# First unit of a two-layer linear-attention kernel: value weight split by ScalarE and GpSimd, film gathered earlier, attention in two column groups

## The reference

```python
xn = _ln(x, ln_w, ln_b)
q = xn @ Wq + bq
k = xn @ Wk + bk + (1.0 - src_mask) * -1000000.0
q = jax.nn.softmax(q.reshape(b, t, h, dh), axis=-1)
k = jax.nn.softmax(k.reshape(b, t, h, dh), axis=1)
v = ((xn @ Wv + bv) * src_mask).reshape(b, t, h, dh)
att = jnp.einsum('bnhd,bnhl->bhdl', k, v)
y = jnp.einsum('bnhd,bhdl->bnhl', q, att).reshape(b, t, d)
emb_out = (jax.nn.silu(emb) @ W_emb + b_emb)[:, None, :]
scale, shift = jnp.split(emb_out, 2, axis=2)
hh = _ln(y, ln2_w, ln2_b) * (1.0 + scale) + shift
hh = jax.nn.silu(hh) @ W_out + b_out
return x + hh
```

## Time and profile before

| what | value |
|---|---|
| median of three runs | 811.47 us (810.06 to 811.48) |
| the profiled execution | 811.12 us |
| its span, first to last instruction | 809.2 us |
| TensorE busy | 766.0 us, 95% |
| VectorE busy | 698.7 us, 86% |
| ScalarE busy | 517.0 us, 64% |
| GpSimd busy | 438.4 us, 54% |
| chain that ended last, by engine | TensorE 80%, VectorE 10%, issue 3%, ScalarE 3%, DMA 2%, GpSimd 1% |
| first unit: start of `attend(0)` | 72.03 us |
| start of `output(0)` | 115.47 us |

### The profile page before, as it was taken

One profiled execution on the slowest core, in us unless ns is written; L12 is line 12 of the kernel. 1 busy time (PEld: TensorE's weight loads), 2 busy tenths in 40 slices (PEclk: granted clock), 3 DMA queues, 4 the chain that ended last, 5 costly groups with the idle time before them and its releaser, 6 DMA issues.

```text
span 809.2 us, 16851 instructions
## 1 busy us (share of the span) xinstructions
PE 766.0 (95%) x6359; PEld 371.6 (46%) x6359; DVE 698.7 (86%) x1421; ACT 517.0 (64%) x1011; POOL 438.4 (54%) x432
## 2 busy tenths in 40 slices
PE   4997979999999999998999999999999999999986
PEld 2445434354444445444454544444454544444442
DVE  6898967798998999999988898888888899888985
ACT  4897763856748687686866685565657476560723
POOL 2475573553856658487563755447265535544352
PEclk9997989999999999999999999999999999999999
DMA  9966497664967759596594939588584939485542
GB/s 320 307 130 187 116 257 220 131 147 135 183 171 139 165 153 183 170 180 173 111 187 119 195 106 175 167 153 200 96 192 117 183 119 182 117 150 139 89 120 79
DMA packets 291201, 130.73 MB, mean 162 GB/s; under 512 B 261392, under 2 KB 261776, under 8 KB 291120
## 3 DMA queue, kind: packets, MB, share of 16 engines
q1 hardware_dynamic: 288384, 125.27, 68.7%
q10 hardware_dynamic: 2736, 4.39, 1.6%
HBM read 47.74 MB, written 16.88 MB: 80 GB/s over the span
## 4 chain that ended last, share of the span: by engine, by line
PE 80%; DVE 10%; issue 3%; ACT 3%; DMA 2%; POOL 1%; SPq 0%; DVEq 0%; ACTq 0%; POOLq 0%
PE ring L529 72%; PE ring L699 3%; PE att_ps L648 2%; DMA sb_ht_parts<-sb_htok 2%; DVE sb_k_or_qt L1021 1%; ACT sb_k_or_qt L1410 1%; DVE sb_q_sum L1080 1%; DVE sb_row_peak L868 1%; DMA sb_x<-in_x 1%; DVE sb_ht_parts L1134 1%; PE att_ps L590 0%; PE film_ps L590 0%; DVE sb_q_max L1054 0%; DVE ring L1051 0%; PE film_ps L599 0%
## 5 line engine op out<-in xcount | busy, mean ns | idle before, releaser
L529 PE MATMUL ring<-sb_w_hi,sb_xt_parts 128*128 128x512 f16 x1024 | 309.0, 379 | 0.0
L529 PE MATMUL ring<-sb_w_lo,sb_xt_parts 128*128 128x512 f16 x512 | 194.0, 379 | 0.0
L529 PE MATMUL ring<-sb_w_hi,sb_ht_parts 128*128 128x512 f16 x512 | 158.3, 384 | 10.0 <-DMA sb_ht_parts<-sb_htok 5.8
L529 PEld LDWEIGHTS ring<-sb_w_hi,sb_xt_parts 128*128 128x128 f16 x1024 | 100.3, 98 | 126.1 <-issue 6.6
L529 PE MATMUL ring<-sb_xt_parts,sb_w_hi 128*128 128x512 f16 x496 | 149.9, 384 | 8.6 <-issue 8.1
L1662 POOL TENSOR_TENSOR sb_htok<-sb_ht_parts,sb_htok 128x512 f16<-128x512 f32 x60 | 75.2, 1275 | 137.7 <-ACT sb_htok L1443 137.7
L1678 POOL TENSOR_TENSOR sb_tanh<-sb_v_or_q,sb_kq_hi 128x512 f16<-128x512 f32 x64 | 74.0, 1157 | 88.2 <-ACT sb_kq_hi L1474 87.6
L529 PE MATMUL ring<-sb_w_lo,sb_ht_parts 128*128 128x512 f16 x256 | 98.3, 384 | 0.0
L529 PE MATMUL ring<-sb_xt_parts,sb_w_lo 128*128 128x512 f16 x248 | 95.2, 384 | 0.0
L529 PEld LDWEIGHTS ring<-sb_w_hi,sb_ht_parts 128*128 128x128 f16 x512 | 50.7, 99 | 71.6 <-issue 9.7
L1467 ACT ACTIVATE sb_v_or_q<-ring,sb_ln_one 128x512 f32<-128x512 f32 x64 | 43.9, 686 | 61.6 <-DVE ring L1056 60.7
(11 more groups left out here) (230 smaller groups left out, 1403.1 us busy)
## 6 DMA issues: line engine op xcount, KB each, us to landing
out<-sb_x SPq DMA_DIRECT2D x14, 1024.0 KB, 4.8
sb_rows_now<-film_rows SPq DMA_DIRECT2D x16, 512.0 KB, 4.4
sb_x<-out SPq DMA_DIRECT2D x8, 1024.0 KB, 5.2
...
```

What stands on the lines that cost most here:

```text
L529: last = nc.tensor.matmul(out, lhs, rhs, start=(n == 0), stop=(n == len(pairs) - 1))
```

## The change

Only the first unit's lists change. V's weight is split as Q's is: ScalarE scales and casts chunks 0 and 1 ahead of the keys' exponents and 2 and 3 behind them, GpSimd makes the low halves, and `split_low(V_)` is gone from VectorE. VectorE folds V's bias and makes `v_scales` ahead of `key_sums`. `turn_film` goes behind value tile 0 and `bound_film` behind value tile 2, with `gather_film` and `film_scales` moved to match; `turn_table` goes ahead of the whole `first_attention`, whose products become two column groups of 64 x 64. `mask_attention` goes ahead of `query_sums`, and `find_scale(0, O_)` and `output_scale(0)` between the two pairs of attended tiles. ScalarE makes query tile 0 whole ahead of `normalise(1)`, which is cut in two; `x_sums(2)` goes behind `copy_table` and `x_squares(2)` behind `high_attention`. GpSimd's `add_bias(0)` goes behind `x_norm(2)`. SP issues the transposes of the queries ahead of those of unit 1's input.

```diff
@@ -332,7 +332,7 @@
...
         w_ready = [sem(f"w_ready{i}") for i in range(LAYERS)]
-        q0_ready, o0_ready = sem("q0_ready"), sem("o0_ready")
+        q0_ready, v0_ready, o0_ready = sem("q0_ready"), sem("v0_ready"), sem("o0_ready")
         consts_ready, emb_tanh_ready, emb_ready, pick_ready = sem("consts_ready"), sem("emb_tanh_ready"), sem("emb_ready"), sem("pick_ready")
@@ -438,8 +438,8 @@
...
                 turn_k(0)
+                turn_q(0)
                 turn_x(0, 0)
-                turn_q(0)
                 turn_x(0, 1)
@@ -664,20 +664,21 @@
...
 
-            def first_attention(between):
+            def first_attention():
 
...
                 for tiles in (range(T - 1), (T - 1,)):
-                    if tiles[0]:
-                        between()
                     pe.wait_ge(v_lo_ready, tiles[-1] + 1)
...
                             for n, (lhs, rhs) in enumerate(pairs):
-                                last = nc.tensor.matmul(att_ps[:, c, :], lhs, rhs, start=(c == t == n == 0), stop=(c == C - 1 and t == T - 1 and n == 2))
+                                for j in range(2):
+                                    g = slice(j * HALF, j * HALF + HALF)
+                                    last = nc.tensor.matmul(att_ps[g, c, g], lhs[:, g], rhs[:, g], start=(c == t == n == 0),
+                                                            stop=(c == C - 1 and t == T - 1 and n == 2))
                 last.then_inc(att_summed, 1)
@@ -718,18 +719,19 @@
...
                 def with_v(i):
-                    if i == 1:
+                    if i == 0:
                         turn_film(0)
-                    elif i == 3:
+                    elif i == 2:
                         bound_film(0)
...
                 project_tokens("Q", 0, Q_, xt_hi, xt_lo, between=with_q)
-                pe.wait_ge(w_ready[0], 8)
+                pe.wait_ge(v0_ready, 2)
                 project_tokens("V", 0, V_, xt_hi, xt_lo, between=with_v)
-                first_attention(between=lambda: turn_table(0))
+                turn_table(0)
+                first_attention()
                 pe.wait_ge(table_copied, 2)
@@ -1134,15 +1136,18 @@
...
 
+            def attended_pair(u, pair):
+                for t in pair:
+                    attended(u, t)
+                for t in pair:
+                    y_statistics(u, t)
+                y_moments(u, pair)
+                for t in pair:
+                    centre(u, t)
+
             def attended_all(u):
-                for pair in ((0, 1), (2, 3)):
-                    for t in pair:
-                        attended(u, t)
-                    for t in pair:
-                        y_statistics(u, t)
-                    y_moments(u, pair)
-                    for t in pair:
-                        centre(u, t)
+                attended_pair(u, (0, 1))
+                attended_pair(u, (2, 3))
 
@@ -1179,29 +1184,29 @@
...
                                                ).then_inc(emb_ready, 1)
-                split_low(V_)
+                fold(0, V_)
+                v_scales(0)
                 key_sums(0)
-                fold(0, V_)
                 queries(0, 0)
...
                 queries(0, 3)
-                v_scales(0)
                 values(0, 0)
+                gather_film(0)
                 values(0, 1)
+                film_scales(0)
                 values(0, 2)
-                gather_film(0)
                 values(0, 3)
-                film_scales(0)
                 find_peak(0, O_)
-                query_sums(0)
                 dve.wait_ge(blocks_loaded, 16)
                 mask_attention(0)
+                query_sums(0)
+                attended_pair(0, (0, 1))
                 find_scale(0, O_)
                 output_scale(0)
-                attended_all(0)
+                attended_pair(0, (2, 3))
 
@@ -1319,20 +1324,20 @@
...
 
-            def scale_and_split(layer, m):
+            def scale_and_split(layer, m, chunks=range(C)):
 
...
                     act.wait_ge(done["K"], 4 * B)
-                if (layer, m) == (0, Q_):
-                    act.wait_ge(shift_part, 2)
-                n = 0 if (layer, m) == (0, Q_) else 4 * (prepared(layer, m) - 3)
-                for c in range(C):
+                if layer == 0 and m != O_:
+                    act.wait_ge(shift_part, folded(0, m))
+                n = 4 * (prepared(layer, m) - 2)
+                for c in chunks:
                     nc.scalar.activation(stages[layer][m][:, c, :], stages[layer][m][:, c, :], ACT.Copy, scale=scale_of(layer, m, c)
                                          ).then_inc(w_scaled, 1)
-                    if c:
+                    if c > chunks[0]:
                         high_weight(layer, m, n, c - 1)
-                high_weight(layer, m, n, C - 1)
+                high_weight(layer, m, n, chunks[-1])
 
@@ -1387,21 +1392,23 @@
...
 
-            def normalise(unit):
+            def normalise(unit, tiles=range(T)):
 
                 act.wait_ge(x_affine_ready, unit + 1)
-                if unit > 1:
+                if tiles[0]:
+                    pass
+                elif unit > 1:
                     act.wait_ge(q_lo_ready, 4 * (unit - 1))
...
                     act.wait_ge(mask_stored, 32)
-                for t in range(T + 1):
-                    if t < T:
+                for t in range(tiles[0], tiles[-1] + 2):
+                    if t <= tiles[-1]:
                         nc.scalar.activation(xh_of(unit)[:, t, :], xt(unit, t), ACT.Identity, bias=x_add[:, t:t + 1],
                                              scale=x_rstd[:, t:t + 1]).then_inc(xh_ready, 1)
-                    if t:
+                    if t > tiles[0]:
                         act.wait_ge(xh_ready, 4 * unit + t)
@@ -1446,6 +1453,8 @@
...
                     act.wait_ge(x_squared, 4 * min(u + 1, LAST))
+                elif u == 0:
+                    act.wait_ge(v0_ready, 2)
                 for t in tiles:
@@ -1510,24 +1519,25 @@
...
                 copy_shift(0, V_)
-                split_high(V_)
+                scale_and_split(0, V_, (0, 1))
                 for i in range(C):
                     exponent_of_keys(0, i)
+                scale_and_split(0, V_, (2, 3))
                 high_keys(0)
-                exponent_of_queries(0, 0)
-                normalise(1)
+                high_queries(0, 0)
+                normalise(1, (0, 1))
                 copy_film(0, 0)
-                halve_queries(0, 0)
+                high_queries(0, 1)
+                high_queries(0, 2)
                 copy_film(0, 1)
-                for t in range(1, T):
-                    high_queries(0, t)
+                high_queries(0, 3)
+                normalise(1, (2, 3))
+                for t in range(T):
+                    high_values(0, (t,))
+                copy_table(0)
                 x_sums(2)
-                high_values(0, (0, 1, 2))
-                x_squares(2, (0, 1))
-                high_values(0, (3,))
-                copy_table(0)
                 high_attention(0)
-                x_squares(2, (2, 3))
+                x_squares(2)
                 load_film_w(1, 0)
@@ -1687,8 +1697,8 @@
...
 
-            def low_weight(layer, m, ready):
-                for c in range(C):
+            def low_weight(layer, m, ready, chunks=range(C)):
+                for c in chunks:
                     pool.wait_ge(w_hi_ready, 4 * prepared(layer, m) - C + c + 1)
@@ -1697,16 +1707,19 @@
...
                 low_weight(0, Q_, q0_ready)
-                pool.wait_ge(w_ready[0], 8)
-                add_bias(0)
-                for t in range(T):
-                    low_x(1, t)
-                low_queries(0)
-                low_values(0, (0,))
+                low_weight(0, V_, v0_ready, (0, 1))
+                low_weight(0, V_, v0_ready, (2, 3))
+                low_queries(0, (0,))
+                low_x(1, 0)
+                low_x(1, 1)
+                low_queries(0, (1, 2, 3))
+                low_x(1, 2)
+                low_x(1, 3)
+                low_values(0)
                 x_mean(2)
-                low_values(0, (1, 2, 3))
                 low_attention(0)
                 x_norm(2)
+                add_bias(0)
                 low_weight(0, O_, o0_ready)
```

## The result

The changed kernel takes 815.61 us (median of six runs, 814.01 to 819.16); the kernel before, on the same chip, 810.93 us (809.91 to 811.49). The ratio is 1.0072, 95% interval 1.0058 to 1.0086: slower by 4.7 us, where 812.3 was forecast and 814.8 was the top of the range.

The account below looks back on a forecast made before the run. TensorE was taken as the bound from unit 2 on, so only `output(0)`'s start counted: -1.6 + 1.6 before `attend(0)`, +1.15 for the chain behind, so 811.12 + 1.2 = 812.3 us, range 809.2 to 814.8.

Parts of the forecast that it names:

- Where the wait arises: TensorE after value tile 0: a new 3.0 us wait for ScalarE's film copies, held by the key transpose.
- The clock: TensorE behind the new gap: 3.4 us at 0.50 on `turn_film` and value tile 1, costing 1.6 us.
- rival D: TensorE's low clock lasts twice as long, 6.7 us: +3.2 instead of +1.6, 813.9 us; chance 0.18.
- the likeliest case: Whole kernel: start of `attend(0)` unmoved, chain behind it 1.15 us longer, 812.3 us (811.3 to 813.6); chance 0.42.
- E + 6.7: Forecast start of `attend(0)`, 6.7 us after the value tiles' end (E, 63.75): 70.45, before the low clock's cost.
- S' + 17.8: Unit 1's key exponents on ScalarE, 17.8 us after `attend(0)`'s new start (S', 72.05); 16.65 before, so 1.15 longer.
- The change touches none of those units: Units from 2 on: TensorE is the bound, and the change only moves when `output(0)` starts.
- the prediction's last sign of being wrong: Units from 2 on would differ in length, which no row led the prediction to expect.
- B: TensorE's clock stays high after the new gap: -0.45 us, 810.7 us, no change; chance 0.15.
- C's first way: Before `turn_film`: film copies are in time, `attend(0)` starts at 67.45, total 807.7 us; chance 0.05.
- Its second way: Before `output(0)`: low `ht_parts` transpose gets further before film weights, up to 5.8 us of gap goes, 806.5; chance 0.15.
- E: As a rival, unit 0's attention: column groups do not run side by side, 4.9 us later, 817.2 us; chance 0.05.

Follow-up runs that it names:

- e2: Changed kernel with 18 extra unread products on TensorE filling the wait ahead of `turn_film`, against the kernel before: 813.9 us, ratio 1.0054.
- e14: e12 with the second film copy moved behind the third query cast on ScalarE, against the kernel before: 810.38 us, ratio 1.0002.
- e4: Changed kernel with `x_sums(2)` behind `high_attention` on ScalarE and `x_mean(2)` behind `low_attention` on GpSimd, against the kernel before: 815.29 us, ratio 1.0081.
- e13: Changed kernel without the column groups, against the kernel before: 815.17 us, ratio 1.0064.
- e3: Changed kernel with the output weight's scale found ahead of the first attended pair, against the kernel before: 817.38 us, ratio 1.0096.
- e7: Kernel before with the two column groups alone, against the kernel before: 807.85 us, ratio 0.9979.
- e11: Kernel before with the column groups and `mask_attention` ahead of `query_sums`, against the kernel before: 807.02 us, ratio 0.996.
- e12: e11 plus the change's film places, keeping ScalarE's old order with both film copies in time, against the kernel before: 806.5 us, ratio 0.9952.
- e1: Changed kernel with ScalarE's film copies moved ahead of query tiles 1 to 3, against the kernel before: 809.84 us, ratio 1.001.

## Why the prediction was wrong

**Where the wait arises: right, 1 us short.** The prediction had ScalarE held until 47.65 for the key transpose; the cast ran at 48.05. The second copy was to end at 54.2 and ended at 54.56; value tile 0 ended at 50.74 instead of 51.24. So 3.96 us of wait in place of 3.0; `turn_film` started 0.45 later than forecast.

**The clock: this is the step that failed first.** The prediction took "a low stretch of 3.4 us", +1.6, by likeness to the stretch behind the old 2.39 us gap. It was 6.8 us, 3.4 lost: rival D, to which 0.18 was given. e2 shows it by itself, 3.6 us at `attend(0)`. The prediction read two low stretches in the trace of before, and took the one whose gap was nearer in length. That trace has a third in the first unit, behind the gap of 1.72 us ahead of `attend(0)` at 72.03:

```profile
71.00:72.00 1.00, 0.00 (x0) 0.00 (x0) 0.93 (x7) 0.92 (x5) 0.54 (x2) 0.74 0.09 16
72.00:73.00 1.00, 0.93 (x18) 0.58 (x18) 0.56 (x4) 1.00 (x3) 1.00 (x3) 0.50 0.21 70
...
78.00:79.00 1.00, 1.00 (x6) 0.39 (x4) 1.00 (x3) 1.00 (x2) 1.00 (x2) 0.85 1.01 387
```

It lasted 6.8 us, from about 71.5 to 78.3, twice as long as the one behind the longer gap of 2.39 us. So the rows at hand showed both lengths behind gaps of about 2 us, the length of the gap alone does not set the stretch (e14's, behind 1.94 us, was 6.8 us too), and rival D deserved at least the chance of the likeliest case. In e4 and e13, which wait as long at the same place, the stretch was even 10.2 us, which no case of the prediction had. With the 6.8 us of the change's trace, though, the clock alone does not carry the time out of the range: with +3.2 the prediction's own sum is 813.9. The terms below had to come with it.

**From the tiles' end to `attend(0)`: right.** E + 6.7 was forecast; it was 74.64 - 67.80 = 6.84. Of the 2.6 us by which `attend(0)` missed 72.05, 0.45 is the start, 1.8 the clock, and the rest small.

**The chain behind: right in kind, short.** Exponents at S' + 17.8 were forecast, S' + 18.46 came; before it was S + 16.65. ScalarE was on time (tanh at 91.93, forecast 91.8). What came last was VectorE's key shift, forecast at S' + 17.6 and ready at S' + 18.4; VectorE's share had been priced 0.8 us too low in small pieces, the largest the product for the gated rows at 89.74, which took 1.57 us beside GpSimd's work where it had taken 0.97 (85.27). e3 shows the same from the other side: ScalarE sooner by 5.3 us gives 0.6. From the exponents to `output(0)` it took 26.6 us, 26.8 before, so there the prediction holds.

**"The change touches none of those units": a term put at nothing, 1.6 us.** The delay grew from 4.3 us at `output(0)` to 5.9 at `attention(2)`, by gaps ahead of unit 2's keys. SP issued the transposes of their input late (`turn_x(1, 0)` at 118.72 against 110.37, 8.35 us). Only 5.1 of these are the delay of the chain; the other 3.2 come from SP's list: the two transposes of the gated rows held SP for 8.85 us where they had held it for 4.64. e13, the change without groups, has 4.68 there, and its delay does not grow (6.9 us at `output(0)`, 6.7 at `attention(2)`). That the hold makes the gaps is argued from these starts: the profile names no releaser for them. Over all traces the stretch from `output(0)` to `attention(2)` is 48.7 to 49.5 us in the five with a hold under 5 us, and 49.4 to 50.7 in the twelve with about 9. e7, e11 and e12 have the long hold too, so it does not come from the late copy; what sets it is open. The prediction had followed only the rows of unit 0 to the end of unit 1.

With all these sizes the sum would have been 811.12 + 5.9 = 817.0; the medians differ by 4.7. In the two traces the delay is 5.9 us until `attention(6)`, 4.1 at `attention(7)` and 2.5 at `attention(15)` (775.99 against 773.50). The first 1.8 is the gap with the low clock at 371.70, which the trace of before has and that of the change has not; the rest comes in small steps behind `attention(8)`. So the prediction's last sign of being wrong, that units from 2 on differ in length, also came true, and the net of it made the miss smaller: without it the time would have lain further outside the range. That part is chance and not foresight.

**The rivals.** D happened. B fell with the rows. C's first way, copies in time, is e1's trace up to `attend(0)` (67.85 where 67.45 was worked out), though the time came out as 809.84, not 807.7. Its second way fell: the gap before `output(0)` grew, from 5.81 to 7.22, as the likeliest case had it. E fell: the groups run side by side, 96 halves in 1.85 us.
